# Attention: query and key biases as column operands of ACT and DVE instead of a matmul

## The reference

```
Q = split_heads(x @ Wq.T + bq)          # 16 heads of 8
K = split_heads(x @ Wk.T + bk)
V = split_heads(x @ Wv.T + bv)
scores = einsum('bhqd,bhkd->bhqk', Q, K) / sqrt(8) + prior_lambda * mask
out = einsum('bhqk,bhkd->bhqd', softmax(scores), V)
return merged(out) @ Wo.T + bo
```

## Time and profile before

| | us |
|---|---|
| median of 3 runs (lowest to highest) | 1100.94 (1098.42 to 1102.85) |
| the profiled execution | 1097.69 |
| its span, first to last instruction | 1095.9 |
| PE busy in the span | 924.6 (84%) |
| DVE busy | 906.8 (83%) |
| ACT busy | 707.2 (65%) |
| mean granted clock of PE | 0.951 of full |

### The profile page before, as it was taken

One profiled execution on the slowest core, in us unless ns is written; L12 is line 12 of the kernel. 1 busy time (PEld: TensorE's weight loads), 2 busy tenths in 40 slices (PEclk: granted clock), 3 DMA queues, 4 the chain that ended last, 5 costly groups with the idle time before them and its releaser, 6 DMA issues.

```text
span 1095.9 us, 37172 instructions
## 1 busy us (share of the span) xinstructions
PE 924.6 (84%) x13792; PEld 636.5 (58%) x13792; DVE 906.8 (83%) x2396; ACT 707.2 (65%) x1370; POOL 611.1 (56%) x672
## 2 busy tenths in 40 slices
PE   3475867999899989999999898999898999886882
PEld 3364734558655568556755585555585555673671
DVE  6788857988899997897499978999888999865676
ACT  2262655667866677867865778666678666776681
POOL 6571555553364445554755465465375555557775
PEclk9896876999999999999999999999999999998897
DMA  8512539245422265224922373222374115463744
GB/s 276 162 46 32 121 100 288 71 85 127 121 66 64 55 107 161 70 70 93 219 63 71 92 170 87 63 63 65 72 160 118 60 62 134 80 160 101 161 111 112
DMA packets 205390, 118.88 MB, mean 108 GB/s; under 512 B 107264, under 2 KB 195938, under 8 KB 204960
## 3 DMA queue, kind: packets, MB, share of 16 engines
q1 hardware_dynamic: 189856, 89.40, 32.9%
q0 software_dynamic: 15360, 27.10, 9.7%
HBM read 35.33 MB, written 62.42 MB: 89 GB/s over the span
## 4 chain that ended last, share of the span: by engine, by line
DVE 42%; PE 35%; issue 12%; ACT 7%; DMA 2%; POOL 2%; DVEq 0%; SPq 0%; ACTq 0%; POOLq 0%
DVE row_max L1607 15%; DVE h_lo L1498 5%; PE banks L717 5%; PE banks L746 3%; PE banks L509 3%; PE banks L692 3%; PE banks L602 2%; DVE stats L1287 2%; DVE x_all L1489 2%; PE banks L563 2%; PE banks L604 2%; PE banks L565 2%; PE banks L564 2%; PE banks L605 2%; PE banks L497 2%
## 5 line engine op out<-in xcount | busy, mean ns | idle before, releaser
L1010 ACT ACTIVATE probs<-banks 128x512 f32<-128x512 f32 x512 | 278.2, 597 | 164.4 <-PE banks L717 164.2
L1089 POOL DMA_INDIRECT xg<-xs,slots x240 | 248.3, 1035 | 196.0 <-PE banks L717 88.9
L1607 DVE TENSOR_REDUCE row_max<-banks 128x2 f32<-128x512 f32 x512 | 334.0, 684 | 26.9 <-PE banks L717 19.0
L1103 POOL DMA_INDIRECT big<-yg,slots x240 | 242.3, 1010 | 142.3 <-PE banks L717 52.9
L1498 DVE TENSOR_TENSOR h_lo<-h_f,h_hi 128x512 bf16<-128x512 f32 x208 | 141.2, 687 | 66.5 <-ACT h_hi L924 63.4
L602 PE MATMUL banks<-w_all,h_hi 128*128 (+1 forms) x832 | 157.0, 222 | 44.5 <-DVE h_lo L1498 42.9
L746 PE MATMUL banks<-probs,v_op 128*32 128x256 f32 x2048 | 183.0, 387 | 4.8 <-ACT ot_sb L1003 3.1
L922 ACT ACTIVATE h_f<-banks 128x512 f32<-128x512 f32 x208 | 125.2, 602 | 83.3 <-PE banks L565 80.0
L717 PE MATMUL banks<-band_parts,thirds 96*32 96x296 bf16 (+2 forms) x4096 | 174.6, 278 | 0.0
L692 PE MATMUL banks<-q_op,k_op 32*128 32x256 bf16 x1024 | 138.7, 277 | 20.7 <-issue 7.6
L604 PE MATMUL banks<-w_all,h_hi 128*128 (+1 forms) x832 | 153.6, 222 | 0.1
(11 more groups left out here) (188 smaller groups left out, 1697.5 us busy)
## 6 DMA issues: line engine op xcount, KB each, us to landing
yg<-y_rows SPq DMA_DIRECT2D x84, 256.0 KB
q_in<-kq_kept SPq DMA_DIRECT2D x96, 64.0 KB
k_op<-kq_kept SPq DMA_DIRECT2D x96, 64.0 KB
xg<-zeros SPq DMA_DIRECT2D x2, 2944.0 KB, 10.4
xg<-zeros SPq DMA_DIRECT2D x2, 2432.0 KB, 14.5
kq_kept<-kq_hi SPq DMA_DIRECT2D x32, 128.0 KB
kq_kept<-kq_lo SPq DMA_DIRECT2D x32, 128.0 KB
xg<-xs,slots POOLq DMA_INDIRECT x240
```

The source lines that it names most:

```text
L1010: act.activation(probs[:, q % 2, u % 4, :], banks[:, ST[u % 2], :], ACT.Exp).then_inc(A["exp_done"], 1)
L1089: pool.indirect_dma_start(xg[q], bass.IndirectOffsetOnAxis(slots[:, q % 4, c, t:t + 1], 0), xs[:, NTH[q] % 2, t, :], None, bounds_check=CA ...
L1103: pool.indirect_dma_start(y_back[:, i, c, :], None, yg[q], bass.IndirectOffsetOnAxis(slots[:, q % 4, c, t:t + 1], 0)).then_inc(gathered[i] ...
L1607: dve.tensor_reduce(row_max[:, gp, :, qt, j], banks[:, MX[(16 * b + v) % 3], :].rearrange("p (k c) -> p k c", k=2), AX.X, ALU.max).then_in ...
```

## The change

The query and key biases are no longer added by PE. They are loaded as columns, one value for each partition, and ACT and DVE take them as an operand: ACT makes the high part as Identity with a bias, DVE makes the low part as (bank + bias) - high part. An operand column holds one value for each partition, and the two halves of the bank have different biases, so each engine does it in two operations of 256 columns. The output's bias stays with PE, in a tile of its own.

```diff
-        bias_rows = sb("bias_rows", [P, 3, D])
+        bias_col = sb("bias_col", [P, 2])
+        bo_b = sb("bo_b", [P, D])
-        bias_parts = sb("bias_parts", [P, 3, D], BF16)
+        bo_parts = sb("bo_parts", [P, D], BF16)
...
-            sp.dma_start(bias_rows[:, 0, :], bq.broadcast_to([P, D])).then_inc(attn_in, 16)
-            sp.dma_start(bias_rows[:, 1, :], bk.broadcast_to([P, D])).then_inc(attn_in, 16)
+            sp.dma_start(bias_col[:, 0:1], bq.rearrange("o d -> d o")).then_inc(attn_in, 16)
+            sp.dma_start(bias_col[:, 1:2], bk.rearrange("o d -> d o")).then_inc(attn_in, 16)
...
-                        pe.wait_ge(bias_ready, 1)
...
-                    pe.matmul(o.rearrange("p (t c) -> p t c", t=KT), bias_parts[:, which, :], bc(three_rows[:], 1, KT),
-                              start=False, stop=False)
...
-                act.activation(kq_hi[:].rearrange("p w c -> p (w c)"), banks[:, M[0], :],
-                               ACT.Copy).then_inc(A["kq_hi_ready"], 1)
+                for which in range(2):
+                    i = act.activation(kq_hi[:, which, :], banks[:, M[0], bass.ts(which, L)], ACT.Identity,
+                                       bias=bias_col[:, which:which + 1])
+                i.then_inc(A["kq_hi_ready"], 1)
...
+                        dve.wait_ge(attn_in, 192)
                         key_constants()
...
+                dve.tensor_scalar(bias_col[:, 0:1], bias_col[:, 0:1], QSCALE, None, ALU.mult)
...
-                done(dve.tensor_scalar(bias_rows[:, 0, :], bias_rows[:, 0, :], QSCALE, None, ALU.mult))
-                done(dve.tensor_copy(bias_parts[:], bias_rows[:]))
+                done(dve.tensor_copy(bo_parts[:], bo_b[:]))
                 for r in range(0, 96, 32):
                     dve.memset(three_rows[r:r + 1, :], 1.0)
-                done(dve.tensor_tensor(bias_rows[:], bias_rows[:], bias_parts[:], ALU.subtract))
-                dve.tensor_copy(bias_parts[32:33], bias_rows[32:33])
-                done(dve.tensor_copy(bias_parts[64:65], bias_rows[64:65]))
-                dve.tensor_tensor(bias_parts[64:65], bias_rows[64:65], bias_parts[64:65],
-                                  ALU.subtract).then_inc(bias_ready, 1)
+                done(dve.tensor_tensor(bo_b[:], bo_b[:], bo_parts[:], ALU.subtract))
+                dve.tensor_copy(bo_parts[32:33, :], bo_b[32:33, :])
+                done(dve.tensor_copy(bo_parts[64:65, :], bo_b[64:65, :]))
+                dve.tensor_tensor(bo_parts[64:65, :], bo_b[64:65, :], bo_parts[64:65, :], ALU.subtract)
...
-                dve.tensor_tensor(kq_lo[:].rearrange("p w c -> p (w c)"), banks[:, M[0], :],
-                                  kq_hi[:].rearrange("p w c -> p (w c)"), ALU.subtract).then_inc(A["kq_ready"], 1)
+                for which in range(2):
+                    i = dve.scalar_tensor_tensor(kq_lo[:, which, :], banks[:, M[0], bass.ts(which, L)],
+                                                 bias_col[:, which:which + 1], kq_hi[:, which, :], ALU.add, ALU.subtract)
+                i.then_inc(A["kq_ready"], 1)
```

More of the change, by code:

```diff
@@ L316, in build @@
         high_ready = sem("high_ready")
-        bias_ready = sem("bias_ready")
         waits_met = sem("waits_met")
@@ L373, in _ @@
                 sp.dma_start(wstage[:, n, :], w).then_inc(attn_in, 16)
-            sp.dma_start(bias_rows[:, 0, :], bq.broadcast_to([P, D])).then_inc(attn_in, 16)
-            sp.dma_start(bias_rows[:, 1, :], bk.broadcast_to([P, D])).then_inc(attn_in, 16)
+            sp.dma_start(bias_col[:, 0:1], bq.rearrange("o d -> d o")).then_inc(attn_in, 16)
+            sp.dma_start(bias_col[:, 1:2], bk.rearrange("o d -> d o")).then_inc(attn_in, 16)
             sp.dma_start(bv_b[:], bv.broadcast_to([P, D])).then_inc(attn_in, 16)
-            sp.dma_start(bias_rows[:, 2, :], bo.broadcast_to([P, D])).then_inc(attn_in, 16)
+            sp.dma_start(bo_b[:], bo.broadcast_to([P, D])).then_inc(attn_in, 16)
             sp.dma_start(lam_b[:], lam.broadcast_to([P, 1])).then_inc(attn_in, 16)
@@ L842, in turn @@
                                 pe.matmul(o, o_hi[:, bass.ts(t, P)], wo_lo[:], start=False, stop=False)
-                                pe.matmul(o, three_rows[:], bias_parts[:, 2, :], start=False, stop=False)
+                                pe.matmul(o, three_rows[:], bo_parts[:], start=False, stop=False)
                                 mm = pe.matmul(o, o_lo[:, bass.ts(t, P)], wo_hi[:], start=False, stop=True)
```

## The result

The changed kernel took 1105.25 us (median of 8 runs, 1101.81 to 1107.40), beside 1101.06 for the kernel before on the same chip (8 runs, 1098.42 to 1102.85). The ratio is 1.0046, with an interval of 1.0032 to 1.006: 5.1 us more, between 3.5 and 6.6. The prediction was 5.0 more. The size came out as forecast, but not each of its terms, as the turns and the start will show.

A forecast was written before the change was run, and what follows sets the result against it. No engine alone bounds it: DVE 42% of the chain, PE 35%, ACT 7%. Kind A 3.1 and 0.06, B 1.35, C 1.7, expert block -0.22, start -1.0 gave +5.0 us, 1105.9 against 1100.94; range 1099.5 to 1110.

The forecast's parts named there:

- PE, -0.22 a turn: Each projection loses two matmuls of 256 columns at 0.11 us, so kq_done comes 0.22 us earlier.
- ACT, 0.87 for the pair, +0.27: At kq_hi, one 0.597 us Copy becomes two Identity operations with a bias column, together 0.87 us, +0.27.
- The dear column: Rival at ACT's kq_hi: one pointer costs all 0.21 us, kq_hi +0.48, sum +9.7 us, 1110.6; chance 0.25.
- DVE, 0.82 to row_max, +0.21: At kq_lo, one subtraction becomes two scalar_tensor_tensor of 256 columns, 0.82 us up to row_max, +0.21.
- the rival of 7.1 us: At kq_lo, DVE's second half starts only when the first ended: pair 0.89, sum +7.1 us, 1108.0; chance 0.07.
- Kind A: 13 turns whose chain goes PE, kq_hi, kq_lo: +0.26 us each in 12, +0.06 in that at 158 us.
- Kind B: 9 turns where the chain goes from the projection straight into PE's scores: +0.15 us each, together 1.35.
- kind C: 8 turns where the chain reaches kq_lo from DVE's earlier work, kq_hi already there: +0.21 us each, together 1.7.
- The start, -1.0: DVE's preparation of the bias rows at the start gets shorter: -1.0 us at most, nothing if a later stage waits.
- the projection in the expert block, -0.22: The one projection of 32 in the first expert block: 0.22 us less.
- The cheap halves: Rival: splitting costs only +0.06 on ACT and +0.05 on DVE, sum -4.4 us, 1096.5; chance 0.15, 0.05 of it faster.

The follow-up runs named there:

- the enlarged constants: Changed kernel with DVE's cast of the output bias row at the start made 26 times instead of once: 1.0116 times the kernel before.
- columns without split: Changed kernel with one 512-column operation on ACT and one on DVE, each with the query's bias column: 0.996, again 0.9976 times the kernel before.
- the kernel without columns: Kernel before without its bias matmuls, ACT and DVE each in two operations of 256 columns with no bias column: 0.9967 times the kernel before.

## Why the prediction was right, and where it was not

**PE, -0.22 a turn.** Right on the chain (six matmuls at 0.11). Alone it is worth 0.16 in a turn, since waits behind it open.

**ACT, 0.87 for the pair, +0.27.** Measured 0.84, +0.25. Half of L908's two operands, 0.105, was the guess for a column; it is 0.09. The Trainium skill, ScalarE: Activation LUTs, section What ACT_TABLE_LOAD costs, gives about 93 ns; 0.473 less 0.384 on 256 columns and 0.687 less 0.597 on 512 agree with it. The dear column, the rival of 9.7 us, began at 0.12 and did not come.

**DVE, 0.82 to row_max, +0.21.** Measured 0.79, +0.18; the form of L1465 was the right row to go by. The second half starts 0.40 behind the first, whose length is 0.476: it does not wait for the first's end. So the rival of 7.1 us falls. The Trainium skill, VectorE: DVE Perf Modes, section The DRAIN you can't avoid, says that the next op does not start until the pipe is empty, which the prediction weighed as that rival, and then that a next op that is not held starts earlier than that. These two agree with the second sentence: 0.40 against 0.476.

**Kind A, +0.26 a turn.** This step failed in size: 0.15. Of the difference, 0.05 is the smaller pairs, and 0.05 the wait between o_n and row_max, which the prediction had as no part of the path. Twelve turns make 1.8 instead of 3.1. DVE's longer wait for kq_hi, "about 0.05", was right: 0.43 instead of 0.37 to 0.40.

**Kind B, +0.15, and kind C, +0.21.** Measured 0.15 and 0.18. Kind B is like kind A in every kernel here, to 0.03 us. Its mechanism was right: PE had no wait for row_max at 241 us and has one of 0.22 after. The middle that was taken between -0.22 and +0.26 was no middle but what both kinds pay.

**The start, -1.0, and the projection in the expert block, -0.22.** The mechanism was right, by the enlarged constants, by the 1.4 and 1.1 us of columns without split, and by the 1.25 between kernels at the same half clock. In the two profiled executions of the changed kernel 0.2 was left of it, because the half clock around that projection took about 1.0, a term that the sum did not have.

**Not in the sum: the clock at 245 us, +1.26.** No step of the prediction asked what a later ACT and DVE do to PE's idle time where an expert block follows, nor what the granted clock does there.

Together: turns 4.7 instead of 6.2, start -0.2 instead of -1.2, clock +1.26: 5.8, where 5.0 was forecast and 5.1 and 6.6 were measured. So the right total is in part luck: it rests on errors against each other, turns that cost 1.5 less than forecast and two stretches at half clock, about 1.0 and 1.26, that were not forecast. The cheap halves, the rival of -4.4, have their mechanism in the kernel without columns, 0.06 and 0.06 for the split; with a column in each half it can't be had.

## What to carry to other kernels

Before a matmul is traded for operand columns, count the operations that get a column, not the bytes or the PE time: here each one cost 0.09 us on ACT and 0.06 on DVE, and one operation with one column on each engine won where two with a column each lost. It could be one, because a key bias, or any constant in its place, only shifts all scores of a row, and the softmax takes that out. Look at the granted clock where a changed turn borders on a stretch that PE fills: in four executions of four a few tenths of a microsecond on other engines, with PE's shorter pass, went with a loss of 1.26 us there.

## What was not expected of the hardware

A column operand and a split each cost the same with and without the other, to 0.01 us, on both engines. TensorE's granted clock fell at one place in four of four executions with the two pairs and the shorter pass, and in none of ten of other shapes, among them the kernel before and the one with that one projection as before. The same idle time of 1.23 to 1.24 us ahead of it was followed by the half clock in the one case and the full clock in the other.
